# Second cross attention of a six-block decoder: another order of score groups, transposes and gates

## The reference, cut to what matters

```
q = einsum('bqa,ahc->bqhc', x, q_weights) * 64 ** -0.5
k = einsum('bka,ahc->bkhc', ctx, k_weights)
v = einsum('bka,ahc->bkhc', ctx, v_weights)
weights = softmax(einsum('bqhc,bkhc->bhqk', q, k) + bias)
weights = where(mask, weights, 0)
avg = einsum('bhqk,bkhc->bqhc', weights, v)
gate = sigmoid(einsum('bqa,ahc->bqhc', x, g_weights) + g_bias)
x = layernorm(x + einsum('bqhc,hco->bqo', avg * gate, o_weights) + o_bias)
```

## Time and profile before

| what | before |
|---|---|
| median of 3 runs | 2049.35 us (2049.07 to 2049.59) |
| profiled execution: span from first to last instruction | 2047.6 us |
| profiled execution: own time beside the span | not recorded |
| PE busy | 1760.9 us, 86% of the span |
| DVE busy | 1414.1 us, 69% |
| ACT busy | 1030.3 us, 50% |
| POOL busy | 450.5 us, 22% |
| granted TensorE clock, mean | 0.928 |

### The profile page before, as it was taken

The page is one execution under the profiler, slowest core; times in us unless marked ns, Lnnn a source line. Parts: engine busy times, 40 slices in busy tenths (PEclk is TensorE's granted clock), DMA queues, the critical chain, the costliest instruction groups (busy, mean ns, idle before and its releaser), DMA issues.

```text
span 2047.6 us, 34996 instructions
## 1 busy us (share of the span) xinstructions
PE 1760.9 (86%) x12889; PEld 1262.8 (62%) x12889; DVE 1414.1 (69%) x4997; ACT 1030.3 (50%) x2596; POOL 450.5 (22%) x493
## 2 busy tenths in 40 slices
PE   3678888888788779999999999998879999989808
PEld 1357666666653456666667766666648998974307
DVE  7887888886136977777775676776546666653685
ACT  6545556555347535555553455555125455443752
POOL 4000000000000233333333333333212332320003
PEclk7779888889789979999999999999899999999959
DMA  5000000000001010000000000000413433400001
GB/s 158 1 1 1 1 1 1 1 2 2 1 1 41 21 67 2 1 1 1 1 2 1 1 1 2 1 1 1 137 35 90 94 67 90 94 1 0 0 0 41
DMA packets 86079, 49.57 MB, mean 24 GB/s; under 512 B 40223, under 2 KB 83669, under 8 KB 85717
## 3 DMA queue, kind: packets, MB, share of 16 engines
q1 hardware_dynamic: 80195, 47.18, 8.9%
q10 hardware_dynamic: 5714, 0.16, 0.2%
HBM read 45.24 MB, written 2.10 MB: 23 GB/s over the span
## 4 chain that ended last, share of the span: by engine, by line
PE 61%; DVE 27%; ACT 7%; issue 3%; POOL 2%; POOLq 0%; DVEq 0%; ACTq 0%
PE PS L1694 7%; PE PS L1721 6%; PE PS L1995 6%; DVE nx L764 6%; DVE sq L773 6%; PE PS L1708 5%; PE PS L1679 3%; PE PS L1666 3%; PE PS L2413 3%; PE PS L2058 3%; PE PS L1736 2%; PE PS L2014 2%; PE PS L2023 2%; PE PS L1655 2%; DVE nnm L1149 2%
## 5 line engine op out<-in xcount | busy, mean ns | idle before, releaser
L1760 ACT ACTIVATE px<-PS,cnm 128x128 f32<-128x128 f32 (+7 forms) x256 | 189.3, 740 | 261.8 <-DVE cnm L1808 254.9
L1851 POOL TENSOR_SCALAR px<-px,crl 128x128 f32<-128x128 f32 (+7 forms) x128 | 225.9, 1765 | 412.3 <-DVE crl L1823 412.3
L773 DVE TENSOR_SCALAR sq<-nx 128x4 f32<-128x4 f32 x1024 | 175.4, 171 | 31.4
L764 DVE TENSOR_TENSOR_SCAN nx<-sq 128x6 f32<-128x6 f32 x1024 | 173.9, 170 | 32.0 <-POOL sq L903 0.9
L1805 DVE TENSOR_REDUCE cm<-PS 128x1 f32<-128x128 f32 (+6 forms) x224 | 154.2, 689 | 55.0 <-PE PS L1694 54.5
L1708 PE MATMUL PS<-ident,px 128*128 128x128 f32 x1152 | 158.9, 279 | 15.0 <-ACT qT L1748 9.5
L1708 PEld LDWEIGHTS PS<-ident,px 128*128 128x128 f32 x1152 | 129.9, 141 | 61.9 <-issue 34.7
L1721 PEld LDWEIGHTS PS<-pT,V 128*64 128x64 f32 x2304 | 124.8, 137 | 63.7 <-issue 34.6
L1694 PE MATMUL PS<-kT,qT 64*128 64x512 f32 (+3 forms) x768 | 159.0, 519 | 5.0 <-ACT px L1760 2.6
L1721 PE MATMUL PS<-pT,V 128*64 128x128 f32 x2304 | 154.7, 279 | 5.9 <-DVE pT L1816 2.3
L198 POOL TENSOR_SCALAR rstd<-mv 128x1 f32<-128x1 f32 x80 | 34.2, 427 | 534.3 <-DVE mv L176 534.3
(11 more groups left out here) (338 smaller groups left out, 3839.3 us busy)
## 6 DMA issues: line engine op xcount, KB each, us to landing
xbs<-in_fside_Bx16xSxS SPq DMA_DIRECT2D x8, 1232.0 KB, 6.7
fsrc<-in_fside_Bx16xSxS SPq DMA_DIRECT2D x8, 1232.0 KB, 6.6
xmk<-in_mask_Bx16xSxS_bk SPq DMA_DIRECT2D x8, 308.0 KB, 8.7
fsrc<-in_mask_Bx16xSxS_bk SPq DMA_DIRECT2D x8, 308.0 KB, 8.4
X<-in_x SPq DMA_DIRECT2D x4, 512.0 KB, 6.8
w<-in_L_attn_W_ffn SPq DMA_DIRECT2D x2, 1024.0 KB, 12.9
t<-in_L_ffn_w SPq DMA_DIRECT2D x2, 1024.0 KB, 11.8
out<-xs SPq DMA_DIRECT2D x16, 128.0 KB, 1.7
```

Source lines behind the costliest of these rows:

```text
L764: e.tensor_tensor_scan(k.nx[:, t % 2, :], d0, d1, 0.0, ALU.mult, ALU.add).then_inc(sem("rec.scan"), 1)
L773: e.tensor_scalar(place(c % 2 * 2 * W6 + 6 * n + 7), state, 10.0, -10.0, ALU.min, ALU.max).then_inc(sem("rec.clip"), 1)
L1760: e.activation(k.px[n % 2][:, h, 0:width], src, ACT.Exp, scale=-1.0, bias=k.cnm[:, n % 4, h:h + 1], accum_out=k.cl[:, n % 4, h:h + 1]).the ...
L1851: e.tensor_scalar(k.px[n % 2][:, 0, 0:width], k.px[n % 2][:, 0, 0:width], k.crl[:, n % 4, 0:1], None, ALU.mult).then_inc(sem("c.normal0"), 1)
```

## The change

In each pass the first two score groups follow one another directly; the third moves from before the value product to directly behind its tail. Gates and transposes of the old tile are put in another order between them, the second gate half moves behind the transposes of the layer normalization. The table of banks is set anew to fit. No instruction is added or removed.

```
@@ cross_order
         if new:
-            o.add(("x.score", g, 0))
-        if old:
-            o.add(("x.gate", g - 1, 0), ("x.turn", g - 1, 2), ("x.turn", g - 1, 3))
-        if new:
-            o.add(("x.score", g, 1))
+            o.add(("x.score", g, 0), ("x.score", g, 1))
         if g > 1:
             o.add(("unit", 6, g - 2))
         if old:
-            o.add(("x.gate", g - 1, 1), ("x.turn", g - 1, 4))
+            o.add(("x.turn", g - 1, 2), ("x.gate", g - 1, 0), ("x.turn", g - 1, 3), ("x.turn", g - 1, 4))
         if new:
-            o.add(("x.score", g, 2), ("x.normal", g, 0))
+            o.add(("x.normal", g, 0))
         if g > 1:
             o.add(("turn", 6, g - 2), ("put", 6, g - 2), ("f.tile", g - 2))
         if old:
-            o.add(("x.mix", g - 1, 0), ("x.mix", g - 1, 1))
+            o.add(("x.gate", g - 1, 1), ("x.mix", g - 1, 0), ("x.mix", g - 1, 1))
+        if new:
+            o.add(("x.score", g, 2))
@@ CROSS_BANKS
-CROSS_BANKS = {("x.turn", 0): 4, ("x.turn", 1): 5, ("x.gate", 0): 6, ("x.turn", 2): 4, ("x.turn", 3): 5, ("x.gate", 1): 4,
-               ("x.turn", 4): 5, ("x.mix", 0): 6, ("x.mix", 1): 5, ("x.query", 0): 4, ("x.query", 1): 6}
+CROSS_BANKS = {("x.turn", 0): 4, ("x.turn", 1): 5, ("x.turn", 2): 4, ("x.gate", 0): 6, ("x.turn", 3): 5, ("x.turn", 4): 4, ("x.gate", 1): 5,
+               ("x.mix", 0): 6, ("x.mix", 1): 4, ("x.query", 0): 5, ("x.query", 1): 6}
```

## The result

The changed kernel takes 2068.48 us (median of 4 runs, 2068.32 to 2068.72) against 2049.21 for the kernel before in the same comparison: ratio 1.0096, 95% interval 1.0082 to 1.0111. That is 19.3 us slower, where 20.8 were forecast. The profiled span went from 2047.6 to 2066.9 us, by the same 19.3.

What follows compares the result with a forecast made beforehand. PE bounds the kernel at 19.43 us a pass; after the change a 20.68 us ring through DVE, ACT and POOL does. 1.3 + 16.3 (13 x 1.25) + 3.2 = 20.8 us more, about 2070.0 us, range 2059 to 2077.

Steps and rivals of the forecast that it cites:

- the ring over DVE, ACT and POOL: Loop of waits in a second cross attention pass, from one residual step r to the next: 20.68 us.
- Part 1: PE's own sum per pass: five array-shape switches instead of nine, 0.18 us each, so 18.70 us instead of 19.43.
- rival A: PE stays the bound and gets faster: each of 13 periods 0.72 us shorter, total 2038.7 us; chance 0.09.
- Part 2: Waits through DVE, ACT and POOL make the period 20.68 us, 1.25 more; PE idles about 2 us per pass.
- the value that was chosen: DVE's second mask product taken as 1.39 us; with 1.57 the period would be 20.86, the total 2.3 us higher.
- Part 3: Gate half 1, layer normalization's steps, scaled queries and the fetch on SP move at no cost.
- Part 4: Ends of the loop: first pass 1.3 us later, r of tile 14 and last pass together 3.2 us more.
- The opening: First pass: r of tile 0 comes 1.3 us later, by the same new pieces as in the periodic part.
- The end: Last pass: gate half 0, 1.98 us long, fills 1.2 us of existing PE waits and adds 0.8 us.
- rival C: PE's clock falls because of new idle time: 1.7 us in each of 13 passes, total 2092 us; chance 0.04.
- 13 periods: The repeating passes of the loop, each 1.25 us longer, 16.3 us together.
- r of tile 14: Residual step near the loop's end, already waiting for POOL: its 18.3 us becomes a full 20.68, 2.4 more.

Runs made afterwards that it cites:

- the two runs: Two reordered kernels, POOL's bias add early, against the kernel before: six shape switches, 2036.97 us (0.9937); five switches with a list per engine, 2036.56 us (0.9932).
- the run with the first scores apart: Kernel before reordered: first scores after transposes 0 and 1, second before value product, third behind tail, bias add early; 2036.97 us, ratio 0.9937.

## Why the prediction was right

**Sign, size and mechanism** are as forecast: 2068.5 for 2070.0, by the ring over DVE, ACT and POOL. Its links, forecast and measured in the rows above:

| link | forecast | measured |
|---|---|---|
| r to first maximum | 2.19 | 2.20 |
| three maxima, hop | 0.89 | 0.89 |
| 12 exponentials | 4.92 | 4.90 |
| tanh, hop to PE | 1.21 | 1.16 |
| value product | 1.90 | 1.90 |
| tail until gating | 1.20 | 1.19 |
| gatings | 1.20 | 1.20 |
| two maxima, hop | 0.65 | 0.59 |
| four exponentials | 1.76 | 1.77 |
| mask product, hop | 1.58 | 1.59 |
| POOL's scalings | 2.35 | 2.35 |
| bias add, hop to r | 0.83 | 0.83 |
| sum | 20.68 | 20.57 |

**Part 1.** 18.70 for PE alone was right: 18.65 when nothing else is late. A switch is worth 0.19 to 0.20 us where 0.18 was taken; the 24 scores in one go take 1.77 us, which leaves 0.15 by the prediction's 0.0675 for each. In the changed kernel itself PE's busy time was to be about 18.7 and is 18.96 of 20.60. This difference was not taken apart; the ends of matmuls ahead of a wait are modelled. The Trainium skill (TensorEngine Tiling (Array Packing), Key Properties) says that a change of tiling mode drains TensorE; the two runs agree, with 0.19 us as the price here, and show no such price between tail and scores, which have one mode. By this rule alone the change would have been rival A. The two fastest kernels, with other orders, end about 2 us below what rival A named (2038.7), helped by a first pass that is some 3 us shorter; the change itself doesn't come near it.

**Part 2.** The waits on PE came where they were put: 1.26 us ahead of transpose 4 (1.6 forecast) and 0.37 ahead of the value product (0.3 to 0.4). The second mask product took 1.39 us, the value that was chosen.

**Part 3.** The moved parts that were costed at nothing do not appear in the chain of the changed kernel's periodic passes. That holds for the fetch too: no wait for a load is in the list of waits from 1555 to 1800 us.

**Part 4** was wrong in both halves, and the errors partly cancel. *The opening*: r of tile 0 was to be 1.3 us later and came 0.4 earlier (1554.72 for 1555.08). The step that failed took the first pass to be a pass like the others. Before, the second mask product of tile 0 ran beside POOL's scalings of the first half, and PE's first transposes waited for them. These are rows of the kernel before, which the prediction had not used:

```profile
1530.29 1.89 POOL L2174 TENSOR_TENSOR YT<-YT,xrl 128x1024 f32<-128x1024 f32 x1 [12.74 <-DVE YT L2136]
...
1530.45 3.03 DVE L2136 TENSOR_TENSOR YT<-YT,xmk 128x1232 f32<-128x1232 f32 x1
...
1532.15 1.74 POOL L2175 TENSOR_TENSOR fsrc<-YT,xrl 128x208 f32<-128x208 f32 x1
...
1533.94 1.84 PE L2023 MATMUL PS<-ident,YT 128*128 128x128 f32 x8 [4.97 <-POOL fsrc L2175]
```

The mask product and POOL's second scaling were stretched (3.03 for 1.39, 1.74 for 0.54). After, with the third maxima behind the first mask product, they hardly meet (0.08 us), and PE's first transposes start 1.27 us earlier, 1.20 of it from POOL's second scaling. The Trainium skill (GPSIMD Engine Reference, section 8, Key points) has this contention for VectorE instructions with two SBUF inputs, and the durations agree:

```profile
1532.08 0.54 POOL L2173 TENSOR_TENSOR fsrc<-YT,xrl 128x208 f32<-128x208 f32 x1
...
1532.54 1.39 DVE L2134 TENSOR_TENSOR YT<-YT,xmk 128x1232 f32<-128x1232 f32 x1
...
1532.67 1.97 PE L2021 MATMUL PS<-ident,YT 128*128 128x128 f32 x8 [3.77 <-POOL fsrc L2173]
```

From these transposes to r it took 21.14 us before and 22.05 after. So the new pieces did cost in the first pass, 0.91 for the 1.3 forecast, and the earlier start outweighed them.

*The end*: from the last but one r to the last, 15.6 us were forecast (14.79 before, and 0.8) and 18.12 measured. The order of the blocks is the forecast one, but they ran at half clock:

```profile
1844.35 1.09 PE PS L2021 x4
1845.43 3.41 PE PS L1993 x16
1848.85 1.50 PE PS L2021 x8
...
1850.56 1.98 PE PS L1993 x16
```

A gate half took 3.41 us where the next one took 1.98. The first transposes took 1.09 for 0.64 in the last pass of the kernel before, the other eight instructions 1.50 for 0.87. Together that is about 2.5 us, and 18.12 less 2.5 is the forecast 15.6: the step that failed is the clock, put at full speed for the last pass. This is rival C's mechanism, in one pass in place of all: PE had been idle from 1840.1 to 1844.35, for 4.2 us, longer than any wait that it had in the periodic passes. The granted clock was 0.82 in the 5 us before 1845 and 0.50, the lower level of 1.2 GHz, in the 5 us after.

In sum: opening -0.4 (forecast 1.3), 13 periods 14.8 (16.3), r of tile 14 2.2 (2.4), last pass 3.3 (0.8): 19.9 by the last r. The stages behind it were 0.6 us shorter, for a reason that was not looked into. That the total came so close, 19.3 for 20.8, is partly luck: the errors are -1.7, -1.5, -0.2 and +2.5, and -0.6 behind the loop. Most of the total, 14.8, is the ring, and there the forecast was 0.12 us off in each of 13 periods. A slip of addition beside it: 2049.35 and 20.8 are 2070.15, not 2070.0.

## What to carry to other kernels

Where an engine is busy all the time, a block taken from its list pays only if every ring of waits through the other engines stays shorter than the list; add the rings up from starts in the trace of before, hops included, over one whole period. Moving a step in a list that all engines walk moves it on each of them. The two runs that turned a change of +19 us into one of -13 keep what PE waits for (the first tanh, the copies of the transposes) from standing behind a row of 12 exponentials or maxima, and POOL's add early. A place for each engine's part is one way to do it; the run with the first scores apart came within 0.4 us of it with one common list, but for POOL's bias add. A wait that is seen in every pass may cost nothing, so test it by the chain that ended last, or by an edit and its control.

## What the runs showed of the hardware that was not expected

- Where VectorE's product of two SBUF tiles met GpSimd's scalings, one was held up by the other in turn, and they did not share evenly. The scaling that had started first kept its 1.89 us; the product that started 0.16 us behind it took 3.03 for 1.39, and the next scaling 1.74 for 0.54. All three were over in 3.60 us, where their lengths alone add up to 3.83. A product that met a scaling for only 0.28 us took 1.57.
- Idle time of TensorE of 1.3 and 0.4 us in each of 14 passes left the granted clock at 1.00, from 1555 to 1842 us; one idle time of 4.2 us was followed by 5 us at 0.50, and then by 1.00 again.
- A switch of the array's shape cost 0.20 us where three of nine were removed and 0.19 where four were, and between two blocks of the same shape, tail and scores, there was none (0.53 us for eight score instructions, no leftover).
